# VectorE takes all four low parts of the second half of x in each step; GpSimd keeps those of the first half

## What is computed

```python
# layer 0 (adapter ids itok_B_3_7), then layer 1 (adapter ids itok_B_4_50)
Bx   = einsum('bni,bri->bnr', x, B[ids])        # rank 16 adapter of each sequence
c    = einsum('bnr,bor->bno', Bx, A[ids])
base = einsum('bth,oh->bto', c, W) + b
gate = softmax(router logits of c)              # 4 experts
lora = sum_e gate_e * 2 * (c @ A_e.T) @ B_e.T   # rank 8 experts
x    = x + base + lora
```

## Time and profile before

| | us |
|---|---|
| median of 3 runs | 347.21 |
| lowest, highest | 346.39, 350.4 |
| the profiled execution, its own time | 347.15 |
| its span, first to last instruction | 344.8 |
| mean granted TensorE clock in it | 0.985 of full |

### The profile page before, as it was taken

One profiled execution on the slowest core, in us unless ns is written; L12 is line 12 of the kernel. 1 busy time (PEld: TensorE's weight loads), 2 busy tenths in 40 slices (PEclk: granted clock), 3 DMA queues, 4 the chain that ended last, 5 costly groups with the idle time before them and its releaser, 6 DMA issues.

```text
span 344.8 us, 6569 instructions
## 1 busy us (share of the span) xinstructions
PE 321.4 (93%) x2109; PEld 301.4 (87%) x2109; DVE 245.3 (71%) x503; ACT 148.8 (43%) x314; POOL 87.4 (25%) x70
## 2 busy tenths in 40 slices
PE   6798489889999999999999999999999999999975
PEld 5697479778999999899998999999998999999864
DVE  4848984897587848685868766966787587845554
ACT  5768762841356216620664065504651356203210
POOL 3460000461026203540245005600461026200000
PEclk9999969999999999999999999999999999999989
DMA  7999970004780377117920794059504880140014
GB/s 278 380 367 406 332 232 0 0 2 130 257 281 6 97 240 274 63 55 251 281 84 10 223 311 125 0 167 310 192 0 122 257 288 3 61 185 0 0 58 187
DMA packets 30997, 56.17 MB, mean 163 GB/s; under 512 B 3537, under 2 KB 20482, under 8 KB 30978
## 3 DMA queue, kind: packets, MB, share of 16 engines
q1 hardware_dynamic: 29634, 51.41, 45.0%
q0 software_dynamic: 1344, 4.52, 3.4%
HBM read 39.15 MB, written 16.78 MB: 162 GB/s over the span
## 4 chain that ended last, share of the span: by engine, by line
PE 58%; issue 12%; DVE 8%; SPq 7%; POOL 5%; DMA 5%; ACT 3%; POOLq 0%; ACTq 0%
PE ps_d L304 13%; PE ps_d L306 13%; PE ps_d L305 13%; POOL xs_lo L917 5%; DMA xraw<-x_in 2%; DVE k_lo L668 2%; PE ps_h L311 2%; SPq L239 2%; PE ps_p L304 2%; PE ps_t L432 2%; SPq L241 2%; PE ps_p L306 2%; PE ps_p L305 2%; DVE ps_s L879 2%; DMA abraw<-ab_tab 2%
## 5 line engine op out<-in xcount | busy, mean ns | idle before, releaser
L917 POOL TENSOR_TENSOR xs_lo<-xraw,xs_hi 128x512 fp32r<-128x512 f32 x46 | 63.2, 1383 | 187.6 <-ACT xs_hi L505 187.5
L304 PE MATMUL ps_d<-w1s_hi,a1s_hi 128*128 128x384 f32 (+1 forms) x216 | 72.1, 334 | 2.3 <-DVE w1s_lo L668 2.3
L306 PE MATMUL ps_d<-w1s_hi,a1s_lo 128*128 128x384 f32 (+1 forms) x216 | 70.2, 325 | 0.0
L305 PE MATMUL ps_d<-w1s_lo,a1s_hi 128*128 128x384 f32 (+1 forms) x216 | 69.9, 324 | 0.0
L903 DVE SCALAR_TENSOR_TENSOR xraw<-ps_d,bsum,xraw 128x512 f32<-128x512 f32 x62 | 46.2, 749 | 27.0 <-PE ps_d L306 27.0
L505 ACT ACTIVATE xs_hi<-xraw 128x512 fp32r<-128x512 f32 x64 | 38.3, 623 | 15.3 <-DMA xraw<-x_in 9.0
L304 PEld LDWEIGHTS ps_d<-w1s_hi,a1s_hi 128*128 128x128 f32 x216 | 41.0, 190 | 3.0 <-DVE w1s_lo L668 2.6
L305 PEld LDWEIGHTS ps_d<-w1s_lo,a1s_hi 128*128 128x128 f32 x216 | 41.1, 190 | 0.4
L304 PE MATMUL ps_p<-xs_hi,bst_hi 128*128 128x256 f32 x128 | 37.5, 293 | 3.7 <-POOL xs_lo L917 1.7
L306 PEld LDWEIGHTS ps_d<-w1s_hi,a1s_lo 128*128 128x128 f32 x216 | 40.9, 189 | 0.0
L505 ACT ACTIVATE hsb<-hsb 128x32 f32<-128x32 f32 x8 | 1.8, 230 | 84.8 <-DVE hsb L688 82.3
(11 more groups left out here) (165 smaller groups left out, 694.1 us busy)
## 6 DMA issues: line engine op xcount, KB each, us to landing
out<-xraw SPq DMA_DIRECT2D x32, 512.0 KB, 3.5
xraw<-x_in SPq DMA_DIRECT2D x28, 512.0 KB, 5.2
abraw<-ab_tab SPq DMA_DIRECT2D x64, 128.0 KB, 2.1
b0raw<-b_tab SPq DMA_DIRECT2D x64, 64.0 KB, 1.9
w_plain<-w SPq DMA_DIRECT2D x8, 512.0 KB, 9.8
xraw<-w SPq DMA_DIRECT2D x4, 512.0 KB, 6.0
xraw<-w POOLq DMA_DIRECT2D x4, 512.0 KB, 6.8
xraw<-x_in POOLq DMA_DIRECT2D x4, 512.0 KB, 8.6
```

The lines of the kernel that those rows point to most:

```text
L304: pe.matmul(acc, lh, rh, start=first, stop=False, skip_group_check=True)
L305: pe.matmul(acc, lh, rl, start=False, stop=False, skip_group_check=True)
L306: return pe.matmul(acc, ll, rh, start=False, stop=final, skip_group_check=True)
L917: return pool.tensor_tensor(dst, whole, high.bitcast(F32), ALU.subtract)
```

## The change

VectorE makes the low parts of all four chunks of the second half: chunks 0, 1 and 2 in front of `softmax(1)`, chunk 3 within it, where it was. GpSimd makes the four chunks of the first half and then `a1s_lo`. The values that TensorE waits for are changed to fit: `x_lo` is now raised four times for each step, and so is `x_lo_dve`. The high parts, the products and the buffers are the same.

```diff
--- before.py
+++ after.py
@@ -334,11 +334,9 @@
                     if isinstance(g, int) and g == 0:
                         pe.wait_ge((x_lo, x_first_lo)[half], kc + 1)
                     elif half == 0:
-                        pe.wait_ge(x_lo, 6 * g - 2 + kc + 1)
-                    elif kc % 2 == 0:
-                        pe.wait_ge(x_lo, 6 * g - 2 + CH + kc // 2 + 1)
+                        pe.wait_ge(x_lo, CH * g + kc + 1)
                     else:
-                        pe.wait_ge(x_lo_dve, 2 * g - 2 + kc // 2 + 1)
+                        pe.wait_ge(x_lo_dve, CH * g - CH + kc + 1)
                     for k in range(KC * kc, KC * (kc + 1)):
                         cols = tuple(t[:, k, 2 - 2 * half:4 - 2 * half, :].rearrange("p a n -> p (a n)")
                                      for t in bst)
@@ -709,7 +707,7 @@
                     low(xs[1][:, KC * i:KC * (i + 1), :], xraw[0][:, KC * i:KC * (i + 1), HALF:],
                         xs[0][:, KC * i:KC * (i + 1), :]).then_inc(x_first_lo, 1)
 
-            def split_x_odd(g, par, chunks):
+            def split_second_x(g, par, chunks):
 
                 for i in chunks:
                     dve.wait_ge(x_hi, 2 * CH * g + CH + i + 1)
@@ -841,7 +839,7 @@
                                       mx[:].rearrange("p (j a) -> p j a", a=1).to_broadcast([P, TT, EXP]),
                                       ALU.subtract).then_inc(sm_step, 1)
                     if layer == 1 and not last:
-                        split_x_odd(g + 1, 1 - par, [3])
+                        split_second_x(g + 1, 1 - par, [3])
                     dve.wait_ge(exp_done, 2 * g + layer + 1)
                     dve.tensor_reduce(rs[:, 0, :], ex[:], AX.X, ALU.add).then_inc(sm_step, 1)
                     dve.wait_ge(sm_step, at + 4)
@@ -887,7 +885,7 @@
                     low(k2[1][L1ROWS[half], cols], cm[L1ROWS[half], cols], k2[0][L1ROWS[half], cols]
                         ).then_inc(c1_lo, 1)
                 if not last:
-                    split_x_odd(g + 1, 1 - par, [1])
+                    split_second_x(g + 1, 1 - par, [0, 1, 2])
                 if last:
                     wide_low(2)
                 softmax(1)
@@ -945,7 +943,6 @@
             def body(g, par, last):
                 if not last:
                     split_x(g + 1, 1 - par, 0, range(CH))
-                    split_x(g + 1, 1 - par, 1, (0, 2))
                     split_a(g + 1)
 
             steps(pool, body)
```

## The result

| | before | after |
|---|---|---|
| median of 20 executions, us | 347.19 | 344.98 |
| lowest | 345.65 | 343.54 |
| ratio, with its 95% interval | | 0.9933 (0.9912 to 0.9953) |
| the profiled execution, us | 347.15 | 343.93 |
| its span | 344.8 | 342.1 |

The change makes the kernel faster by 0.7%, some 2.3 us. I had forecast 346.9, no change. A second measurement of the same kernel gave 0.9956 (0.9925 to 0.9988). The ratio leaves out four slow executions of the changed kernel, at 349.25 to 349.94 us; with all 20 of each, the medians differ by 2.2 us and the means by 1.6 (347.35 and 345.78).

What follows compares the result with a forecast made beforehand. TensorE, busy 321.4 of 344.8 us, was taken to bound the kernel, with VectorE's list reaching the transposes together with it. 6 x 0.06 - 0.6 = -0.2 us against 347.15 gave 346.9; range 345.3 to 349.5.

Steps and rivals of the forecast that it cites:

- The working of VectorE's list: Steps 1 to 6, read in step 4: softmax starts at 219.32 instead of 219.02, ends at 221.64 instead of 221.58.
- no overlap: Rival: each of three chunks on VectorE costs 0.72 us, not 0.60; +2.25 us, 349.4 in all; chance 14%.
- the change does not free VectorE: Rival: GpSimd's first-half chunk still hinders k2's low parts; 0.82 us a step, +4.3 in all, 351.5 us; chance 3%.
- TensorE's wait ahead of chunk 3: Second projection, steps 1 to 6: chunk 3 comes late, so TensorE waits some 0.2 us.
- Every sign that was named for being right: `k_lo` 0.42, no wait ahead of `route`, chunks 0.60 apart, `lg` 0.18, wait of 0.2 at chunk 3, steps 36.2 to 36.3.
- The hand-over at the transposes: End of softmax to TensorE's transposes: 0.20 us, 221.58 to 221.78 before and 221.64 to 221.84 after.
- the hand-over at `route`: From the end of VectorE's `k_lo` to TensorE's `route`: 0.14 us, leaving VectorE at most 0.06 to spare at the transposes.
- six steps at +0.06: Steps 1 to 6: the softmax and transposes come 0.06 us later, so each step is 0.06 longer.
- Step 0: First step, without GpSimd's last two chunks: reduction 0.76 us sooner, transposes 0.63 sooner, say 0.6; bounds 0.3 and 1.0.
- the sum: Whole run: 6 x 0.06 - 0.6 = -0.2 us, which is no change.
- Against the profiled execution's own 347.15 that is 346.9: Whole run: -0.2 us taken from the profiled execution's 347.15 us gives the forecast of 346.9 us.
- TensorE keeps its 0.31: Rival: steps 1 to 6 each gain the whole wait ahead of `route`; 2.5 us in all, 344.7 us; chance 7%.

Runs made afterwards that it cites:

- all_four_first: The changed kernel with chunk 3 also in front of softmax(1); its steps took 36.43 to 36.60 us, in the main 36.57.
- steps1to6_only: The kernel before with the change in steps 1 to 6 alone, step 0 as before; steps 1 to 6 took 36.33, 36.22, 36.19, 36.23, 36.22, 36.10 us.
- after_again: The changed kernel, unchanged, measured once more for the spread; ratio to before 0.9956 (0.9925 to 0.9988).
- the two filled kernels: Kernels before and after, each with ten unread products in TensorE's pauses of the last step; ratios 0.9975 and 0.9946, mean spans 344.30 and 343.77 us.

## Why the prediction was wrong

**The steps.** The working of VectorE's list came out to 0.03 us: counted from the mask, the first chunk starts at 2.74 us (I had 217.52 - 214.80 = 2.72), the reduction at 4.55 (4.52), chunk 3 at 5.35 (5.33), the softmax ends at 6.87 (6.84). The three chunks lie 0.60 to 0.62 apart, so the first rival, *no overlap*, did not come, and neither did *the change does not free VectorE*. TensorE's wait ahead of chunk 3 is 0.20, as forecast. Every sign that was named for being right came, but for the steps, which took 36.1 to 36.2 where I had 36.2 to 36.3.

**The hand-over at the transposes** was mis-sized. I added 0.20 to the end of the softmax. The transposes start 0.06 behind it (220.07 + 0.29 = 220.36, 220.42), and in all_four_first too. The 0.14 was the hand-over at `route`, and it does not hold here. So VectorE had 0.14 to spare before, not 0.06: it was TensorE that came last to the transposes, and a step is 0.05 shorter up to them instead of 0.06 longer. With steps 2 to 6 unchanged within 0.07 each and 0.04 longer together, six steps at +0.06 was 0.3 to 0.4 too much; step 1 is 0.23 shorter, which steps1to6_only did not repeat.

**Step 0** gave 0.80 instead of 0.63; the reduction came 0.76 sooner, as worked out, the same hand-over makes the rest.

Together the schedule gave 1.0 in this pair of profiles (0.9 with after_again's, 0.7 between the two filled kernels) where the sum had 0.2. That alone would have given 346.2, inside my range.

**The step that failed** is the last of the sum: "Against the profiled execution's own 347.15 that is 346.9". It takes it that what is not changed costs what it cost. The row of PEclk in the page of before ends in "89" and the stretch 330 to 336 was granted 0.72; I used the clock only for the middle of the run (1.00 in the earlier trace rows) and put what it does elsewhere at nothing, without a reason. In the profile after, the pauses of the last step come 1.24 us sooner and the clock does not fall behind them. In the two profiles that is worth 1.46 us, more than the whole schedule; in the mean over executions less, since each kernel has both kinds, and how much less these runs do not tell. None of the rivals has it: *TensorE keeps its 0.31* named 344.7, near the measured time, but by luck, for a reason that steps1to6_only refutes, steps of 35.9.

What share of the measured gain (2.3 us, and 1.5 in the second measurement) is the clock's isn't settled better than that: about 1 us is the schedule's (0.7 to 1.2, by the masks and at equal clock); the rest goes with the clock, and why the clock falls or does not stays open.

## What to carry to other kernels

Where an engine waits for another, count the list in front of the semaphore that both reach together, not the single wait: here a wait of 0.31 us was removed from each of six steps for nothing, and a chunk less on the list gave 0.2. Before adding up, look at every fall of the granted clock in the profile, also outside the change, and ask what a shift of a microsecond would do to it; a few matmuls in a pause, whose products nobody reads, can hold the clock (in the last step of five profiles out of five, where it was worth 1.3 to 1.5 us). A gain of under 1% should be read at equal clock, execution by execution, before it is put down to the schedule.

## What the runs showed of the hardware

Behind the same two pauses of TensorE, of 1.14 to 1.17 and 1.38 us, the clock fell to 1.2 GHz in eight profiles and stayed at 2.4 in three; the last step took 21.4 to 21.6 us with the fall and 20.1 without. Whether it falls goes with when the pauses come: 1 of 24 executions had a mean clock of 0.989 or more when all behind step 0 came 1.4 us later, against 18 of 32. What the chip goes by is open.

Subtractions of 128x512 in a row start 0.60 to 0.62 us apart on VectorE, though each lasts 0.68 to 0.69: `xs_lo` x3 in 1.90, x4 in 2.50. Behind an instruction on the other half of the partitions the next one starts 0.03 after its end (216.20, 216.23). The Trainium skill's section "Two Vector instructions with no wait between them" in "VectorE: DVE Perf Modes" has such a rule: an instruction is held until all earlier ones have finished if it starts in another quadrant of partitions than those before it. The trace agrees in both cases. The sentence in the same page's section "The DRAIN you can't avoid" that the next instruction waits for the pipe to empty holds here for the second case alone.

Where GpSimd and VectorE both subtracted two tiles in SBUF at once, GpSimd's chunk took 1.68 to 1.82 us against 1.29, and VectorE's 16-element `lg` up to 0.56 against 0.18: the one that came second waited, whatever its size.
